# Cross attention on one core: keys of four heads made together, and the context product in three high/low passes, one iteration later

## The reference, cut to what matters

```
q = (layernorm(x) @ Wq)  -> 16 heads of 128, rmsnorm over the 128, times gq
k = (ctx @ Wk)           -> 16 heads of 128, rmsnorm over the 128, times gk
v = (ctx @ Wv)           -> 16 heads of 128
a = softmax(q k^T / sqrt(128)) v        per sequence and head
x = x + tanh(g_xattn[1]) * (a @ Wo)
```

## Time and profile before

| what | value |
|---|---|
| median of 3 runs | 1162.65 us |
| the profiled execution's own time | 1166.83 us |
| its span | 1165.0 us |
| TensorE busy | 994.8 us (85%) |
| VectorE busy | 745.4 us (64%) |
| ScalarE busy | 648.9 us (56%) |
| GpSimd busy | 515.7 us (44%) |
| mean granted TensorE clock | 0.933 of full speed |

### The profile page before, as it was taken

The page is one execution under the profiler, slowest core; times in us unless marked ns, Lnnn a source line. Parts: engine busy times, 40 slices in busy tenths (PEclk is TensorE's granted clock), DMA queues, the critical chain, the costliest instruction groups (busy, mean ns, idle before and its releaser), DMA issues.

```text
span 1165.0 us, 15796 instructions
## 1 busy us (share of the span) xinstructions
PE 994.8 (85%) x5573; PEld 802.6 (69%) x5576; DVE 745.4 (64%) x1308; ACT 648.9 (56%) x1261; POOL 515.7 (44%) x513
## 2 busy tenths in 40 slices
PE   5367675557999999999978899988999999999898
PEld 1022232236899998899867788866878888778787
DVE  6799997964555555555526565577565675667575
ACT  3845456674766666677633566723656644343443
POOL 0266550023666666566533344343443544344352
PEclk7579887887999999999989999999999999899999
DMA  9100100007000000000022000000000220000000
GB/s 340 45 1 0 54 1 0 1 23 301 1 1 2 1 1 2 1 2 1 1 105 95 1 1 1 1 1 1 1 1 1 107 97 1 1 1 1 9 11 19
DMA packets 4734, 35.84 MB, mean 31 GB/s; under 512 B 1160, under 2 KB 2192, under 8 KB 3152
## 3 DMA queue, kind: packets, MB, share of 16 engines
q1 hardware_dynamic: 4656, 34.83, 7.7%
HBM read 33.78 MB, written 1.05 MB: 30 GB/s over the span
## 4 chain that ended last, share of the span: by engine, by line
PE 52%; DVE 15%; ACT 6%; issue 5%; DVEq 0%; POOL 0%; ACTq 0%; POOLq 0%
PE psum L377 13%; PE psum L379 12%; PE psum L378 12%; PE psum L604 4%; DVE f_h_lo L1512 4%; PE psum L592 2%; ACT f_silu L1030 2%; PE psum L547 2%; DVE f_silu L1495 2%; DVE x_norm L1072 2%; PE psum L551 1%; DVE f_silu L1504 1%; PE psum L668 1%; PE psum L703 1%; ACT a_P L946 1%
## 5 line engine op out<-in xcount | busy, mean ns | idle before, releaser
L377 PE MATMUL psum<-x_norm_T_hi,f_wgu_hi 128*128 128x512 f32 x400 | 177.7, 444 | 0.0
L1504 DVE TENSOR_TENSOR f_silu<-f_silu,psum 128x512 f32<-128x512 f32 x100 | 68.7, 687 | 165.9 <-ACT f_silu L1030 165.9
L379 PE MATMUL psum<-x_norm_T_hi,f_wgu_lo 128*128 128x512 f32 x400 | 161.2, 403 | 0.0
L378 PE MATMUL psum<-x_norm_T_lo,f_wgu_hi 128*128 128x512 f32 x400 | 160.8, 402 | 0.0
L749 ACT ACTIVATE f_h_hi<-f_silu 128x512 fp32r<-128x512 f32 x100 | 63.0, 630 | 173.1 <-DVE f_silu L1495 172.6
L377 PE MATMUL psum<-f_wd_hi,f_h_hi 128*128 128x256 f32 x400 | 121.7, 304 | 13.2 <-DVE f_h_lo L1512 13.1
L1512 DVE TENSOR_TENSOR f_h_lo<-f_silu,f_h_hi 128x512 fp32r<-128x512 f32 x100 | 123.6, 1236 | 3.6 <-ACT f_h_hi L749 3.5
L1581 POOL TENSOR_TENSOR f_wgu_lo<-f_wa,f_wgu_hi 128x512 fp32r<-128x512 f32 x44 | 56.6, 1286 | 144.7 <-ACT f_wgu_hi L749 144.6
L378 PE MATMUL psum<-f_wd_lo,f_h_hi 128*128 128x256 f32 x400 | 114.2, 285 | 0.0
L379 PE MATMUL psum<-f_wd_hi,f_h_lo 128*128 128x256 f32 x400 | 113.9, 285 | 0.0
L1653 POOL TENSOR_TENSOR m_dBu<-m_du,m_Bs 128x1024 f32<-128x1024 f32 x32 | 77.0, 2409 | 67.6 <-DVE m_du L1170 21.7
(11 more groups left out here) (297 smaller groups left out, 2706.1 us busy)
## 6 DMA issues: line engine op xcount, KB each, us to landing
f_wa<-in_f1a SPq DMA_DIRECT2D x1, 8448.0 KB, 25.2
f_w<-in_f3w SPq DMA_DIRECT2D x1, 5376.0 KB, 17.5
w_raw<-in_w0raw SPq DMA_DIRECT2D x1, 3072.0 KB, 16.4
f_w<-in_f2w SPq DMA_DIRECT2D x1, 3072.0 KB, 14.5
f_wb<-in_f1b SPq DMA_DIRECT2D x1, 2304.0 KB, 8.2
a_wo<-in_wo SPq DMA_DIRECT2D x2, 1024.0 KB, 12.3
a_wq<-in_wq SPq DMA_DIRECT2D x1, 2048.0 KB, 25.0
x_res<-in_x SPq DMA_DIRECT2D x1, 1024.0 KB, 7.3
```

The source lines that it names most:

```text
L377: mm(out, wh, xh, start=start, stop=False, **kw)
L378: mm(out, wh, xl, start=False, stop=False, **kw)
L379: return mm(out, wl, xh, start=False, stop=stop, **kw)
L1504: V.tensor_tensor(sg[g % 2][:, :], sg[g % 2][:, :], ps[:, 3 + 2 * (g % 2), :], ALU.mult).then_inc(S("f_m"), 1)
```

## The change

- **Keys.** One set of three matmuls of 512 columns now makes the keys of four heads for 128 tokens, in bank 7. It has the context as its stationary side and Wk as its moving one, as before, but 512 columns of it. The first iteration makes four such sets, into banks 2 to 5 (a whole group of four heads); the iterations 1 to 28 make one each, and the last three none (`KB` = 29). Keys are scaled into `ktok`, two buffers that each hold a group of four heads for 512 tokens, and transposed from there head by head, still into bank 7. The first set's squares, sums, 1/rms (16 columns) and scaling are four times as large.
- **Context product.** `ctk` and the transposed probabilities are now split too, and the product is 12 matmuls of `mm3` in place of 4 of plain f32. The new low part of the probabilities is `probs_lo` on VectorE, of 128 x 1024. The product of unit i-2 stands in iteration i, after the queries, where that of unit i-1 stood at its end; the output moves from unit i-2 to i-3. `ah` and `al` get a second buffer, and the loop one more iteration.
- **F0.** ScalarE's copies of high parts stand at the start of F0, and are now of ctxT (1024 columns), ctk (1024), all of Wk (2048) and the first two weight parts. GpSimd's low parts of the same follow, ahead of its first `rstd_of`.
- **Transfers.** `f1a` has 10 tiles, `f1b` 18.

```diff
@@ tensor, attn1
+            def keys(i):
+                units = range(TH) if i == 0 else (i + TH - 1,)
+                for n in units:
+                    g, t = n // TH, n % TH
+                    sl = slice((g // 4) * HALF + t * P, (g // 4) * HALF + (t + 1) * P)
+                    wsl = slice((g % 4) * HALF, (g % 4 + 1) * HALF)
+                    last = mm3(ps[:, 2 + t if i == 0 else 7, :], ch[:, sl], cl[:, sl], wkh[:, wsl], wkl[:, wsl], True, True)
+                last.then_inc(S("a_k"), 1)
...
+                if i == 0:
+                    keys(0)
+                    pe.wait_ge(S("xT_ready"), 1)
+                elif i < KB:
+                    pe.wait_ge(S("a_kT"), i)
+                    keys(i)
                 pe.wait_ge(S("a_w"), i + 1)
-                if i:
-                    pe.wait_ge(S("a_kT"), i)
...
-                for t in range(TH):
-                    sl = slice((i // HEADS) * HALF + t * P, (i // HEADS) * HALF + (t + 1) * P)
-                    ksl = slice(t * P, (t + 1) * P)
-                    last = mm3(ps[:, 7, ksl], ch[:, sl], cl[:, sl], hi[:, KC * P:AQ], lo[:, KC * P:AQ], True, True)
-                last.then_inc(S("a_k"), 1)
...
                 if i + 1 < HEADS2:
                     keys_queries(i + 1)
...
+                if 2 <= i <= HEADS2 + 1:
+                    pe.wait_ge(S("a_ptl"), i - 1)
+                    for b in range(2):
+                        for kv in range(2):
+                            last = mm3(ps[:, 4, b * DM:(b + 1) * DM], *(c[:, ((i - 2) // HEADS) * TH + 2 * b + kv, :] for c in (ctkh, ctkl)),
+                                       *(p[:, b, kv * DM:(kv + 1) * DM] for p in (PTh, PTl)), kv == 0, kv == 1)
+                    last.then_inc(S("a_ac"), 1)
...
-                if 1 <= i <= HEADS2:
-                    pe.wait_ge(S("a_pts"), i)
-                    for b in range(2):
-                        for kv in range(2):
-                            last = mm(ps[:, 4, b * DM:(b + 1) * DM], ctk[:, ((i - 1) // HEADS) * TH + 2 * b + kv, :],
-                                      PT[:, b, kv * DM:(kv + 1) * DM], start=kv == 0, stop=kv == 1)
-                    last.then_inc(S("a_ac"), 1)
@@ scalar, ffn0
+            copy(ch[:, :], ctxT[:, :]).then_inc(S("a_ch"), 1)
+            loaded(act, "ctk")
+            copy(ctkh[:, :, :], ctk[:, :, :]).then_inc(S("a_ctkh"), 1)
+            loaded(act, "wq", "wk")
+            copy(wkh[:, :], wk[:, :]).then_inc(S("a_wkh"), 1)
+            parts(0)
+            parts(1)
             inputs(0)
...
-                if t == NT - 2:
-                    copy(ch[:, :], ctxT[:, :]).then_inc(S("a_ch"), 1)
-                    loaded(act, "wq", "wk")
-                    parts(0)
-                    parts(1)
@@ vector, attn1
+            def probs_lo(i):
+                dve.wait_ge(S("a_pts"), i + 1)
+                V.tensor_tensor(PTl[:, :, :], ps[:, 4:6, :], PTh[:, :, :].bitcast(f32), ALU.subtract).then_inc(S("a_ptl"), 1)
...
                 V.scalar_tensor_tensor(nb[:, :], mx[:, :], -1.0, rq[i % 2][:, :], ALU.mult, ALU.mult).then_inc(S("a_nb"), 1)
+                if i:
+                    probs_lo(i - 1)
                 if i + 1 < HEADS2:
                     query_norms(i + 1)
                     keys_lo(i + 1)
```

More of the change, by code:

```diff
@@ L159, in flamingo_kernel @@
     rq = [place("W1", f"a_rq{i}", [P, TH]) for i in range(2)]
+    rks0, rk0 = (place("W1", f"a_{n}0", [P, 4 * TH]) for n in ("k_sum", "rk"))
+    KB = HEADS2 - TH + 1
+    PTl = place("B1a", "a_PT_lo", [P, 2, HALF], f32r)
+    for r, n in ((ah, "hi"), (al, "lo")):
+        r.append(place("B1a", f"a_AC_{n}1", [P, HALF], f32r))
+    voh, vol = ([place("B1a", f"a_wvo_{n}{i}", [P, DM], f32r) for i in range(2)] for n in ("hi", "lo"))
+    ktok = [place("B1a", f"a_k_tok{i}", [P, TH, 4, P]) for i in range(2)]
+    wkh = place("B1a", "a_wk_hi", [P, HEADS * P], f32r)
+    wkl = place("WK", "a_wk_lo", [P, HEADS * P], f32r)
     ch, cl = (place("B1a", f"a_ctxT_{n}", [P, TOK], f32r) for n in ("hi", "lo"))
-    AQ = KC * P + P
+    ctkh = place("B1a", "a_ctx_tok_hi", [P, NT, P], f32r)
+    AQ = KC * P
     awh, awl = ([place("B1a", f"a_w_{n}{i}", [P, AQ], f32r) for i in range(2)] for n in ("hi", "lo"))
-    voh, vol = ([place("B1a", f"a_wvo_{n}{i}", [P, DM], f32r) for i in range(2)] for n in ("hi", "lo"))
     assert at["B1a"] <= at["B1"]
@@ L548, in norm_transpose @@
                 last.then_inc(S("a_qn"), 1)
-                pe.wait_ge(S("a_ktok"), i + 1)
+                pe.wait_ge(S("a_ktok"), min(i + 1, KB))
+                if i >= KB:
+                    pe.wait_ge(S("a_kT"), i)
                 for t in range(TH):
-                    last = nc.tensor.transpose(ps[:, 7, t * P:(t + 1) * P], ktok[:, t * P:(t + 1) * P], ident[:, :])
+                    last = nc.tensor.transpose(ps[:, 7, t * P:(t + 1) * P], ktok[i // 4 % 2][:, t, i % 4, :], ident[:, :])
                 last.then_inc(S("a_kt"), 1)
@@ L894, in squares @@
             def squares(i):
-                act.wait_ge(S("a_k"), i + 1)
+                if i < KB:
+                    act.wait_ge(S("a_k"), i + 1)
                 if i:
                     act.wait_ge(S("a_qn"), i)
-                A(ksq[:, :], ps[:, 7, :], ACT.Square).then_inc(S("a_ksq"), 1)
+                if i == 0:
+                    for b in range(2):
+                        last = A(Pm[b][:, :, :], ps[:, 2 + 2 * b:4 + 2 * b, :], ACT.Square)
+                    last.then_inc(S("a_ksq"), 1)
+                elif i < KB:
+                    A(ksq[:, :], ps[:, 7, :], ACT.Square).then_inc(S("a_ksq"), 1)
                 act.wait_ge(S("a_q"), i + 1)
-                act.wait_ge(S("a_rks"), i + 1)
+                act.wait_ge(S("a_rks"), min(i + 1, KB))
                 A(qsq[:, :], ps[:, 6, :], ACT.Square).then_inc(S("a_qsq"), 1)
@@ L949, in attn1 @@
             norm_T(3, (2, 3), xTh)
+            value_parts(HEADS2 - 1)
             ac_hi(HEADS2 - 1)
@@ L1298, in key_norms @@
                     dve.wait_ge(S("a_rk"), i)
-                V.tensor_reduce(rks[:, :], ksq[:, :].rearrange("p (t d) -> p t d", t=TH), AX, ALU.add).then_inc(S("a_rks"), 1)
+                if i == 0:
+                    for b in range(2):
+                        last = V.tensor_reduce(rks0[:, 8 * b:8 * b + 8], Pm[b][:, :, :].rearrange("p t (c d) -> p (t c) d", c=2), AX, ALU.add)
+                    last.then_inc(S("a_rks"), 1)
+                else:
+                    V.tensor_reduce(rks[:, :], ksq[:, :].rearrange("p (n d) -> p n d", n=4), AX, ALU.add).then_inc(S("a_rks"), 1)
             def queries_lo(i):
@@ L1306, in keys_scaled @@
                 dve.wait_ge(S("a_rk"), i + 1)
[L1307 to L1310 removed]
+                if i == 0:
+                    for b in range(2):
+                        last = V.tensor_tensor(ktok[0][:, 2 * b:2 * b + 2, :, :].rearrange("p t n d -> p (t n) d"),
+                                               ps[:, 2 + 2 * b:4 + 2 * b, :].rearrange("p t (n d) -> p (t n) d", n=4),
+                                               bc(rk0[:, 8 * b:8 * b + 8].unsqueeze(2), [P, 8, P]), ALU.mult)
+                    last.then_inc(S("a_ktok"), 1)
+                else:
+                    g, t = (i + TH - 1) // TH, (i + TH - 1) % TH
+                    if g >= 2:
+                        dve.wait_ge(S("a_kt"), 4 * (g - 1))
+                    V.tensor_tensor(ktok[g % 2][:, t, :, :], ps[:, 7, :].rearrange("p (n d) -> p n d", n=4),
+                                    bc(rk[:, :].unsqueeze(2), [P, 4, P]), ALU.mult).then_inc(S("a_ktok"), 1)
             def query_norms(i):
```

106 lines of the change are left out of this document (57 added, 49 removed).

## The result

The changed kernel takes 1218.05 us (median of 4 runs, 1212.85 to 1226.23) beside 1162.37 us for the kernel before: a ratio of 1.049, with an interval of 1.045 to 1.053. The forecast was 1207 us, with a range of 1182 to 1236.

The account below looks back on a forecast made before the run. TensorE was taken to bound A1's steady part. +26 (period) -0.7 -1.2 (last iterations) +4 -2 (start) +12 (clock) -2 +8 (F0) = +44 us, giving 1207 us on the median, range 1182 to 1236.

Parts of the forecast that it names:

- The sign and the main mechanism: Slower, chance 0.92: in A1 the keys wait for a_kT's round trip of 1.66 us, no longer covered by the context product.
- The waits: In A1's profile after, idle time of 1.8 to 2.2 us before each first key matmul, released by a_kT_lo.
- The period: In A1's steady iterations, 10.7 us in place of 9.64, over 25 iterations +26 us.
- TensorE's clock: In A1, waiting lowers the clock in one of three iterations: +12 us, between bounds of 0 and 37.
- falls in nearly every iteration: Rival for A1: the clock falls in nearly every iteration, +37 in place of +12, 1232 us; chance 0.15.
- F0, GpSimd: At F0's start GpSimd's subtractions hold up VectorE's first quantisation, one instruction each: 8 us late.
- F0, ScalarE: In F0 ScalarE's copies at 239.39 to 241.35 go away, -2.0 us; larger ones at F0's start cost nothing.
- A1's start and end: A1's start: +4 for the larger first keys' chain, -2 for shorter keys; its last iterations: -0.7 and -1.2 us.
- Transfers: In F the larger f1b and the weights queued behind it stay hidden, with 14 us to spare.

Follow-up runs that it names:

- Run 12: Changed kernel with only the keys of four heads made together; context product back behind the keys' transposes, probabilities not split: 1166.80 us, ratio 1.004 to the kernel before.
- run 7: Changed kernel with the VectorE order of run 1, and on TensorE the six query matmuls ahead of the three key matmuls: 1187.80 us.
- run 8: On top of run 7, a_AC_lo ahead of a_k_tok on VectorE: 1171.28 us.
- run 9: On top of run 8, the output product ahead of the context product on TensorE: 1157.09 us.
- run 1: Changed kernel with only VectorE's order changed, the copy of a_q_sum and a_kT_lo ahead of a_PT_lo: 1197.39 us.
- run 5: On top of run 1, 2 unused matmuls ahead of the queries in each iteration, a longer period with the same standstill: 1208.38 us.
- run 6: On top of run 1, 4 unused matmuls ahead of the queries, a longer period with the same standstill: 1219.39 us.
- run 10: Changed kernel with GpSimd's five subtractions of F0 moved behind the fourth tile's quantisation: 1207.37 us.
- run 11: On top of run 9, GpSimd's F0 subtractions moved as in run 10 and cut into pieces of 512 columns: 1148.79 us.

## Why the prediction was right or wrong

*The sign and the main mechanism* were right. The keys follow their transposes directly, and the round trip of a_kT, 1.66 us in the earlier trace rows, stands open in every iteration. The waits are 1.81 to 1.82 (forecast 1.8 to 2.2), released by a_kT_lo, with no gap on VectorE. Run 12 shows that with the old cover the wait is gone, and runs 7 to 9, which keep the new work, that the queries serve as cover as well.

*The period:* 10.7 forecast, 10.62 measured, +24.0 us for +26. a_PT_lo took 1.22 us, as the row of a_max said. That it was on the path for a small part only was right too: the prediction's own sums, 10.7 with it and 10.43 without, differ by 0.27, and run 1 measured 0.26.

*TensorE's clock* is the step that was mis-sized. "I take one in three, between the two: +12" was in fact about two in three: 25 us by TensorE's busy time, and +20.8 net of what the kernel before had lost. The profile before had one standstill of this length with a full iteration behind it, and it was followed by a fall; against it I had set a stretch at the end of A1 with another mix of work. That was the wrong neighbour. The rival "falls in nearly every iteration" had +37. Neither was to be had from one row: between runs 1, 5, 6 and the changed kernel, 0.25 us of standstill or of period goes with 4 to 16 long iterations, so a forecast had to be a range here. The prediction had named this term its weakest.

*F0, GpSimd:* 8 us forecast, the first quantisation ended 9.2 us late (203.93 after a start at 190.17, where before it was 198.42 after 193.89). The mechanism of the earlier trace rows was right, one VectorE instruction held for each of GpSimd's. But three of the four were operations on 4 elements per partition, which stand ahead of the four L1264. I had let the first hold-up begin with L1232 of the earlier trace rows, so that the size came out near with the wrong instructions was in part luck. The Trainium skill ("SBUF — State Buffer", section "Who interferes with whom") says too that tensor_reduce never contends on trn2. The trace of run 10 agrees: L1296 at 230.37, begun beside GpSimd's subtraction, took its usual 1.22 us. (L1258, at 190.17 in the changed kernel, began before GpSimd did and decides nothing.)

*F0, ScalarE:* -2.0 forecast. F0 as a whole is 8.6 us longer, with the quantisation 9.2 late, so no more than 0.6 of it came back there. In run 11, with most of the hold-ups gone, F0 is 1.4 us shorter than before.

*A1's start and end:* +4 - 2 forecast, +3.4 measured up to the keys of unit 3. (GpSimd's power of 16 columns took 2.90 us, where the estimate was 3.5.) The end was to give back 0.7 + 1.2 and cost 1.6 instead: the last context products wait for a_PT_lo too, up to 1.50 us (at 650.99). I had not priced that.

*Transfers:* hidden, as said. F took 561.9 us.

Together: 24.0 + 20.8 + 3.4 + 1.6 + 8.6 - 0.1 = 58.3 us where I had 44. The profiled execution shows 54.5, since M ended earlier, and the medians differ by 55.7. The time stayed inside the range because that had been made wide for the clock, not because the terms balanced: all that were off, but the period's, were off to the same side.

## What to carry to other kernels

Before work is taken off the engine that bounds, look at what that work was covering: an operation that went away or moved may have been all that hid a round trip of other engines, and the saving turns into a wait that is longer than itself. The repair is order, not speed: put whatever doesn't depend on the round trip (here the queries) directly behind its start, then look in the next trace for the loop that binds now; four such changes of order (runs 1, 7, 8 and 9) took 61 us off without touching any arithmetic, a good part of it the clock's. And price the waits of TensorE twice where they recur, once as time and once for the clock.
